# Score stores in four pieces, index spread in three, query norms on GpSimd, a half-array gather and new slot orders

## The reference

```python
h = layernorm(x) * (1 + ca) + sa;  x = x + ga * attention(h)
h = layernorm(x) * (1 + cb) + sb;  x = x + gb * ffn(h)
```

## Time and profile before

| | |
|---|---|
| median of 3 runs | 1554.59 us (1551.76 to 1559.48) |
| the profiled execution | 1558.92 us |
| its span, first to last instruction | 1557.1 us |
| mean granted clock of TensorE, as a share of full speed | 0.964 |
| instructions | 30502 |
| bytes moved by DMA | 36.43 MB |

### The profile page before, as it was taken

How to read it: one execution, slowest core, us unless ns; L and a number is a source line. 1 busy time by engine, 2 the same in 40 slices (tenths; PEclk the granted TensorE clock), 3 DMA queues, 4 the chain that set the end, 5 groups by cost and what they waited for, 6 DMA issues and landing times. The chain is left out here.

```text
span 1557.1 us, 30502 instructions
## 1 busy us (share of the span) xinstructions
PE 1356.1 (87%) x11816; PEld 970.4 (62%) x11816; DVE 923.5 (59%) x3062; ACT 862.4 (55%) x2231; POOL 321.2 (21%) x420
## 2 busy tenths in 40 slices
PE   5889989898897998988898899888899889888797
PEld 4556657576665665665675566656676556566576
DVE  4755585745564756564376576556456665766634
ACT  3344666554644656545574365754665536665483
POOL 0422030201232212200152112020024310302002
PEclk8889999899998999999999999999999899999999
DMA  7121000000102100000011110000001210000000
GB/s 271 50 64 25 9 1 1 1 4 1 49 20 58 28 5 1 1 1 5 8 42 31 54 24 1 2 1 1 4 8 42 73 22 15 1 1 1 1 1 7
DMA packets 41872, 36.43 MB, mean 23 GB/s; under 512 B 31296, under 2 KB 35840, under 8 KB 40192
## 3 DMA queue, kind: packets, MB, share of 16 engines
q1 hardware_dynamic: 41728, 34.49, 7.6%
HBM read 25.46 MB, written 7.44 MB: 21 GB/s over the span
## 5 line engine op out<-in xcount | busy, mean ns | idle before, releaser
L1111 ACT ACTIVATE arena<-ps 128x512 f32<-128x512 f32 (+7 forms) x560 | 252.2, 482 | 231.2 <-PE ps L685 33.5
L547 PE MATMUL ps<-mean_mat 128*128 128x256 bf16 x2038 | 304.6, 283 | 5.8 <-DVE arena L1481 3.0
L547 PEld LDWEIGHTS ps<-mean_mat 128*128 128x128 bf16 x2038 | 192.7, 101 | 97.9 <-issue 56.1
L1897 POOL TENSOR_TENSOR arena<-arena 128x512 f32<-128x512 f32 x64 | 81.2, 1270 | 462.8 <-DVE arena L1494 462.5
L1317 ACT ACTIVATE arena<-arena,small 128x192 f32<-128x192 f32 (+1 forms) x256 | 129.8, 509 | 33.9 <-DVE small L1674 33.4
L1611 DVE TENSOR_TENSOR gath<-ps,rank_tab 96x512 f32<-96x512 f32 x96 | 63.5, 684 | 45.5 <-PE ps L575 45.2
L1722 DVE TENSOR_REDUCE small<-ps 128x4 f32<-128x1024 f32 x64 | 75.3, 1219 | 23.9 <-PE ps L983 23.7
L1775 DVE TENSOR_TENSOR arena<-arena,ps 128x512 f32<-128x512 f32 x64 | 42.9, 686 | 73.1 <-ACT arena L1411 57.9
L1265 ACT ACTIVATE arena<-arena,small 128x224 f32<-128x224 f32 (+1 forms) x128 | 56.6, 444 | 47.2 <-DVE small L1630 47.1
L1474 DVE CUSTOM_DVE_ANT_0 arena<-ps,mask_w_bf 128x192 f32<-128x192 f32 (+1 forms) x256 | 67.4, 320 | 21.2 <-PE ps L661 21.2
L1367 ACT ACTIVATE arena<-ps 128x512 f32<-128x512 f32 x128 | 66.0, 604 | 23.7 <-PE ps L1017 23.5
(11 more groups left out here) (278 smaller groups left out, 2903.4 us busy)
## 6 DMA issues: line engine op xcount, KB each, us to landing
idxb<-idx_scratch SPq DMA_DIRECT2D x8, 1536.0 KB, 6.3
score_scratch<-arena SPq DMA_DIRECT2D x24, 256.0 KB
w_experts<-in_experts SPq DMA_DIRECT2D x3, 1088.0 KB, 16.3
w_wqkv<-in_wqkv SPq DMA_DIRECT2D x1, 1536.0 KB, 8.9
arena<-score_scratch SPq DMA_DIRECT2D x96, 16.0 KB, 2.0
arena<-arena SPq DMA_DIRECT2D x96, 16.0 KB, 1.8
arena<-in_x SPq DMA_DIRECT2D x8, 128.0 KB, 2.2
out_x<-arena SPq DMA_DIRECT2D x8, 128.0 KB, 1.9
```

The costliest lines, as they stand in the source:

```text
L547: mm(to, still[:, 0:P], still, start=True, stop=True)
L1111: return act.activation(dst, src, ACT.Copy)
L1897: ins = pool.tensor_tensor(own, own, turned, ALU.add)
```

## The change

1. **Stores.** Each `gsc` piece is written in four DMAs of 32 partitions instead of one DMA whose DRAM side has the dimensions 4 x 32 x 512.
2. **Indices.** `idxb` is read in three DMAs of 2048 indices per partition, each with a semaphore of its own; `hot[n]` waits for its piece only.
3. **Query norms.** GpSimd's `normed` multiplies q as well as k by the inverse norms; the transposes of q wait for that. `cqs` goes: the exponential has the constant scale 8, the bias is `-8 * mx`.
4. **Half-array gather.** For the last 64 tokens a doubled copy of their latent keys lies on partitions 0 to 63 and 64 to 127 (`kvsrc` gets a third tile, `source` counts modulo 64). The second three matmuls of each of the last four groups use 64 rows, the groups of a pair on different halves; DVE waits for both groups of such a pair.
5. **Orders.** `TURNS` and `BUSY` are new. The counts in `BUSY` add up to 1985 (992 and 993 for the two streams) instead of 2038 (910 and 1128).

```diff
-    c["source"] = (np.arange(P)[:, None] + np.array([[0, P]])).astype(f)
+    c["source"] = np.stack([np.arange(P), P + np.arange(P) % LW], 1).astype(f)
...
-                        sp.dma_start(idxb[:, :], idx_scratch[s:s + 1, :].to_broadcast([P, GT * RANKS]))\
-                          .then_inc(sig(f"idx_spread{s}"), 16)
+                        for n in range(3):
+                            part = slice(LW * RANKS * n, LW * RANKS * n + LW * RANKS)
+                            sp.dma_start(idxb[:, part], idx_scratch[s:s + 1, part].to_broadcast([P, LW * RANKS]))\
+                              .then_inc(sig(f"idx_part{n}{s}"), 16)
...
                         to = score_scratch[s, n, :].rearrange("(m q c) -> q m c", q=4, c=512)
-                        sp.dma_start(to, m.gsc[:, n, :]).then_inc(sig(f"gsc_saved{s}"), 16)
+                        for q in range(4):
+                            sp.dma_start(to[q], m.gsc[32 * q:32 * q + 32, n, :]).then_inc(sig(f"gsc_saved{s}"), 16)
...
-                        sp.wait_ge(*at("gsc_saved", 16 * (n + 1)))
+                        sp.wait_ge(*at("gsc_saved", 64 * (n + 1)))
...
-                    terms = [(m.kv_part[i][:, 0, :], hot[n][:, part]) for i in range(3)]
-                    if n == 2:
-                        terms += [(m.kv_part[i][:, 1, :], hot[3][:, part]) for i in range(3)]
-                    for i, (l_, r_) in enumerate(terms):
-                        last = mm(bank[g % 2][0:GF, :], l_, r_, start=(i == 0), stop=(i == len(terms) - 1))
-                    last.then_inc(*one("gather_mm"))
+                    for i in range(3):
+                        last = mm(bank[g % 2][0:GF, :], m.kv_part[i][:, 0, :], hot[n][:, part], start=(i == 0), stop=(n < 2 and i == 2))
+                    if n < 2:
+                        last.then_inc(*one("gather_mm"))
+                if n == 2:
+                    for i in range(3):
+                        for g in (2 * p, 2 * p + 1):
+                            part = slice(512 * (g % 4), 512 * (g % 4) + 512)
+                            rows_ = slice(64 * (g % 2), 64 * (g % 2) + 64)
+                            last = mm(bank[g % 2][0:GF, :], m.kv_part[i][rows_, 1, :], hot[3][rows_, part], start=False, stop=(i == 2))
+                            if i == 2:
+                                last.then_inc(*one("gather_mm"))
...
-                pe.wait_ge(*at("q_added", 2 * l + k + 1))
+                pe.wait_ge(*at("q_normed", 2 * l + k + 1))
...
                 for j in range(2):
-                    last = mm(bank[2][LW * j:LW * j + LW, 160:192], m.hT[:, L - LW:], w_kv[:, 0:DC], start=True, stop=True)
+                    rows_ = slice(LW * j, LW * j + LW)
+                    mm(bank[2][rows_, 64:128], m.hT[:, P:P + LW], w_kv[:, :], start=True, stop=True)
+                    last = mm(bank[2][rows_, 224:256], m.hT[:, L - LW:], w_kv[:, 0:DC], start=True, stop=True)
...
-                                                     scale=cqs[s][:, T, hh_:hh_ + 1], accum_out=ls[s][:, i, h:h + 1])
+                                                     scale=QK_SCALE, accum_out=ls[s][:, i, h:h + 1])
...
-                dve.tensor_scalar(cqs[s][:, k, :], g[:, 0:H], 8.0, None, ALU.mult).then_inc(*one("rs_final"))
...
-                        dve.wait_ge(*at("gather_mm", g + 1))
+                        dve.wait_ge(*at("gather_mm", g + 1 if p < 4 else 2 * p + 2))
...
-                            dve.scalar_tensor_tensor(nb[s][:, i, :], mx[s][:, i, :], -1.0, cqs[s][:, i // 2, 4 * (i % 2):4 * (i % 2) + 4],
-                                                     ALU.mult, ALU.mult).then_inc(*one("u_bias"))
+                            dve.tensor_scalar(nb[s][:, i, :], mx[s][:, i, :], -QK_SCALE, None, ALU.mult).then_inc(*one("u_bias"))
...
-            def normed_keys(l, k):
+            def normed(l, k):
                 pool.wait_ge(*at("rs_final", 2 * l + k + 1))
-                own = m.own[k][:, 512:].rearrange("p (h n) -> p h n", h=H)
-                pool.tensor_tensor(own, own, bc(rs[s][:, k, H:], 2, DH), ALU.mult).then_inc(*one("k_ready"))
+                for j, name in enumerate(("q_normed", "k_normed")):
+                    own = m.own[k][:, 512 * j:512 * j + 512].rearrange("p (h n) -> p h n", h=H)
+                    pool.tensor_tensor(own, own, bc(rs[s][:, k, H * j:H * j + H], 2, DH), ALU.mult).then_inc(*one(name))
```

More of the change, by code:

```diff
@@ L38 @@
 SCALE_1 = 1.0 / math.sqrt(D1)
+QK_SCALE = 8.0
 ROUTE = 2.826
@@ L422, in program @@
         ssq, rs = ([t[:, 64 + 32 * i:96 + 32 * i].rearrange("p (k n) -> p k n", k=NT) for t in small] for i in range(2))
-        cqs = [t[:, 128:144].rearrange("p (k n) -> p k n", k=NT) for t in small]
         newton = [t[:, 144:160] for t in small]
@@ L1506, in refined @@
                 st.link(dve.scalar_tensor_tensor(nt, nt, -0.5, g, ALU.mult, ALU.mult))
-                st.link(dve.scalar_tensor_tensor(g, nt, 1.5, g, ALU.add, ALU.mult))
-                dve.tensor_scalar(cqs[s][:, k, :], g[:, 0:H], 8.0, None, ALU.mult).then_inc(*one("rs_final"))
+                dve.scalar_tensor_tensor(g, nt, 1.5, g, ALU.add, ALU.mult).then_inc(*one("rs_final"))
             def expert_sum(g):
```

106 lines of the change are left out of this document (52 added, 54 removed).

## The result

The changed kernel takes 1568.2 us (median of 5 runs) where the kernel before takes 1554.6. By the ratio the changed kernel is slower by some 16 us; I had forecast 27 us less, and the time lies outside my range. Its profiled execution took 1562.3 us, the fastest of its runs, with a span of 1560.5.

The account below looks back on a forecast made before the run. No engine's throughput but two streams' wait chains, overlaid in fixed order, bound the kernel. Terms -15 - 3 - 10 - 2 + 9 - 5 + 1 - 2 = -27 us gave 1528 us, range 1504 to 1557.

Parts of the forecast that it names:

- The streams keep their offset: Slot orders made anew: stream 0 gets its attention stage about two slots sooner; value 0, bound 20 us either way.
- they finish inside the same microsecond: PE: second tile's q transposes now wait, first tile's keys queued behind, yet finish in the same microsecond; no separate cost.
- the multiplies: GpSimd also normalises q, so the second tile's keys come 1.09 us later in 16 places: +9 (bounds +4, +17).
- the third rival: Q2 to W0: GpSimd decides; key delays 17 and held-up DVE 35 cost 52 instead of 9: 1571 us, chance 0.14.
- Stores: Score stores in four pieces land after 4.4 us, 1.5 us less per store: -15 (bounds 0 and -30).
- The fixed scale and the tail: ScalarE exponentials with constant scale, 92 ns less each: -10; Newton tail on DVE loses L1508: -2.
- Indices: Index spread in three pieces lets DVE's one-hot build start sooner in 3 of 8 stages: -3, at most 9.
- Half-array gather: PE's last gather matmuls on 64 rows run in pairs, 1.3 us less a sample: -5 (bounds +6 and -10).
- The first: Rival, more than the sum: stalls spread between streams, stores -30 and exponentials -20 nearly in full: 1503 us, chance 0.18.
- The second: Rival, hidden anyway: the other stream's PE work fills what stores leave; only the gather's -5 stays: 1550 us, chance 0.12.
- The fourth: Rival: store pieces run one behind another at the old rate, +17 in place of -15: 1560 us, chance 0.06.
- its sign at the end of the text: Durations as said, span unmoved, PE's fillers and waits grown in A and W slots: the order sets the pace.

Follow-up runs that it names:

- h1: Kernel before, with new slot order and filler counts on PE, ScalarE and DVE only from stream 1's first gather slots to its A2, each round: ratio 1.0139.
- e16: All edits in the old slot orders without moved slots, second root ahead of q's eviction, q's transposes and evictions one slot later: 1.0087 of the kernel before, 1569 us.
- e3: Kernel before with nothing but the score stores in four pieces, in its own orders: ratio 0.9915, 1542.7 us.
- e12: Kernel before with the exponentials' fixed scale and without the last Newton step, q never normalised: ratio 0.9937, 1544 us.
- e4: Kernel before with queries normalised on GpSimd and the fixed scale, in its own slot orders with seven slots moved: ratio 1.0547, 1640 us.
- e20: Kernel before with the fixed scale and GpSimd's 32 multiplies of q added, their product unread, q transposed unnormalised and early: ratio 1.0065.
- e11: Changed kernel, slot orders and all, with only the filler counts of the kernel before: 1.0270 of the kernel before.
- e17: All edits, old orders, q's transposes one slot later, plus 140 more fillers ahead of the waits for q and k: 1.0101 of the kernel before.

## Why the prediction was wrong

**Two steps failed.** The first: "The streams keep their offset ... The rows give no price ... 20 us, is my estimate of the bound, and 0 the value." Measured with the old code, the new slot orders and filler counts are +36 us, where I had 0 for the orders and -2 for the fillers: 38 of the 43 us between my -27 and the +16. Some 22 of the 36 arise where stream 0 enters its attention stage beside stream 1's gather. I had taken just this shift as one that fits the stores. The bound came from the fillers on the chain, and it looked only at idle time that an order can add; it did not see that PE's work for the other stream comes to stand inside a stretch (50 matmuls more in h1's second round), nor that the clock falls with it (1.00 to 0.95 there).

The second is in the query's norm: "the transposes of q (second tile) now wait too, with the first tile's keys queued behind; they finish inside the same microsecond." That was read off the place of k's wait, and the first tile I did not price at all. The transposes of q stood ahead of the norm in PE's order; with the norm before them, 29 of 32 wait 3 us, and the whole engine with them. That is 75 us in the old orders. The changed kernel hardly pays them (12.3 us of waits in 10 places), because its orders move the transposes. It pays for the orders instead. That those were made anew for the norms' sake is my reading and isn't shown; e16 shows that most of the 75 us could be had back by one slot, without them.

**A term too small.** For the multiplies I had +9 (bounds +4 and +17), and for DVE held up beside GpSimd "nothing in the sum, all of it in a rival". Together they measure +20. The mechanism of the third rival is there, in one instruction of each pair of tiles: 13.9 us of DVE time, less than half of the 35 us that it reckoned, and of these a share on the path that wasn't measured.

**Terms that held, and two that gave nothing.** Stores: -15 foretold, -13 measured; but the store took 3.05 us at its best and 3.4 in the median, not 4.4. That is under my lower bound of 3.9, since SP issues the pieces 0.44 us apart and not 0.56, and a piece lands 1.7 us after its issue and not 2.0. So the saving was too low and my share on the path (60%) too high, and that the -15 came so near is in part luck. The Trainium skill's DMA: Bandwidth & Descriptors has, in its section on why a DMA increments its semaphore by 16, that the slowest dimensions of both sides choose the number of engines; its 4 and then 16 go with the 5.85 and 3.05 us and with the DMA share of 0.25 and then 0.48 and 0.53. No run tells more engines for each piece from several pieces under way at once. The Trainium skill's same page gives, in its rules for kernel authors, as the reason against a split that both halves run on all 16 engines already, which the old store did not; so the rule did not bear on this case, and I took it for more than it says. The fixed scale and the tail: -12 foretold, -10 measured, durations to the nanosecond in the changed kernel. Indices: -3 against 0 to 1; of the three stages that I counted the one shown had no wait for the spread, and there the third piece came later than the whole had. Half-array gather: -5 against about +1, within what can be told; PE's time alone was gained, as I had it, but nothing of it shows in the whole.

**The sum as measured.** New orders +36, stores with indices and gather -17 (1.0229 to 1.0117), norms -2 (1.0117 to 1.0101): +16 or so. In those orders the fixed scale's 10 us are all but eaten by what the multiplies and their waits cost. My terms for the norms, -10 - 2 + 9 = -3, are near this -2, but not for my reasons: in the old orders the same edits measure +90.

**The rivals.** The first had -30 for the stores and -20 for the exponentials; they measure -13 and -10. The third gave 1571 us, close to the 1568 measured, but that is luck: by its mechanism the norms alone cost 43 us more than I had, and in the new orders they measure -2. The second, that all is hidden, is refuted by e3 and e12. The fourth is refuted by the 3.05 us. The case that came true had no chance of its own in my list, only its sign at the end of the text.

**What stays open.** Why the new orders lose 11 us outside the gather-side stretch, and 22 inside, is shown by place and by PE's matmuls and clock, not by a single slot; the 11 include the new orders of SP and GpSimd. How much of the 75 us is waiting, how much is fillers that now stand in the way, and how much is the clock that falls with it, was not taken apart; e4's PE is busy 33 us longer than e12's, for the same 11816 matmuls. Orders made for the stores and the fixed scale together, without the norm, weren't tried.

## What to carry to other kernels

Where a value is made later, look first at where its reader stands in the in-order queue of its engine, not at how long the making takes: the wait for the same multiply cost 75 us or, by one slot, some 15 (a difference of sums). An order or a list of fillers made anew is never a free part of a change; run the old code in it, and the new code in the old one, before any edit is priced. Fillers are part of such an order: where a wait moves, they stay behind and stand in the way. And when a bundle comes out slower, try its parts alone: no kernel here was better than the one with one edit of the five.

## What the runs showed of the hardware

Some small DVE instructions that start beside a GpSimd add or multiply end with it. In e4, L1500 takes 0.22 us at 1416.05 and 1.05 at 1421.76, where it ends at 1422.81; the two multiplies of GpSimd end at 1422.78. L1506 takes 1.25 us and ends at 1420.38, an add of GpSimd at 1420.36. In that trace 42 instructions of L1500, L1505 and L1506 start beside one, and each ends 28 to 35 ns after it. Not all are held up: the reciprocal L1459 takes its usual 0.18 us beside a multiply (4 times), and the multiplications with the tables that read PSUM (L1492 to L1494) keep their length. Only the share of these delays that lies on the path counts.

In e12, e20 and e4 the granted clock was the lower, the longer PE had waited for GpSimd's multiply (6.2, 18.7 and 87.3 us), and with it went the time of all that PE does: 0.974, 0.960 and 0.944 for the same number of matmuls, 1349.1, 1360.9 and 1382.3 us busy. The same code and order with 53 more fillers in other places (e11, 0.941, against 0.965 in the changed kernel) was 26 us slower, by the clock and by where the fillers stand together; 140 more of them in e17 were worth nothing.
